# Four groups of hand-set places in a two-layer transformer kernel moved by up to one and a half steps

## The reference

```python
x = x + _L0_attn_ref(_layernorm(x), Mq, Mk, Mv)        # 8 heads, keys of 64, softmax over the queries
x = x + _L0_ffn_ref(_layernorm(x), w_gate, w_up, w_down)  # FP4 quantised inputs and weights, blocks of 16
x = x + _L1_attn_ref(_layernorm(x), w_qkv, ...)        # 16 heads of 16, norm of q and k per head
x = x + _L1_ffn_ref(_layernorm(x), W, b, R, A, B)      # top-2 routing over 8 low-rank experts
```

## Time and profile before

| | us |
|---|---|
| median of 3 runs | 2999.08 |
| lowest, highest | 2991.23, 2999.32 |
| the profiled execution | 2993.89 |
| its span, first to last instruction | 2992.1 |
| TensorE, VectorE, ScalarE, GpSimd busy | 2591.1, 2109.8, 1962.2, 1190.2 |
| HBM traffic over the span | 26 GB/s |
| mean granted TensorE clock | 0.967 of full speed |

### The profile page before, as it was taken

How to read it: one execution, slowest core, us unless ns; L and a number is a source line. 1 busy time by engine, 2 the same in 40 slices (tenths; PEclk the granted TensorE clock), 3 DMA queues, 4 the chain that set the end, 5 groups by cost and what they waited for, 6 DMA issues and landing times.

```text
span 2992.1 us, 115289 instructions
## 1 busy us (share of the span) xinstructions
PE 2591.1 (87%) x50174; PEld 1405.8 (47%) x50174; DVE 2109.8 (71%) x4321; ACT 1962.2 (66%) x3707; POOL 1190.2 (40%) x1677
## 2 busy tenths in 40 slices
PE   4766777999889988899889988899889988899697
PEld 3434554344644456444553456444553446444233
DVE  6778866766778478775778577785788667775433
ACT  2541355776668856787668766787668766687684
POOL 3653156224652166323652155421672246411210
PEclk9987999999999999999999999999999999999798
DMA  4212332324424252323423253152423243222310
GB/s 127 54 27 46 66 70 69 61 48 78 100 64 82 41 113 60 65 63 69 101 74 62 41 92 97 49 85 52 108 63 72 48 85 86 59 66 46 87 30 16
DMA packets 470171, 203.65 MB, mean 68 GB/s; under 512 B 283000, under 2 KB 459648, under 8 KB 469640
## 3 DMA queue, kind: packets, MB, share of 16 engines
q1 hardware_dynamic: 467960, 194.07, 31.3%
q10 hardware_dynamic: 1680, 1.85, 0.2%
HBM read 46.61 MB, written 32.51 MB: 26 GB/s over the span
## 4 chain that ended last, share of the span: by engine, by line
PE 43%; DVE 26%; issue 7%; ACT 7%; SPq 7%; DMA 6%; POOL 3%; DVEq 0%; POOLq 0%; ACTq 0%
PE pR L457 18%; PE pV L688 9%; DVE nmaxa L1215 7%; PE pS L457 6%; PE pS L648 5%; ACT ub L936 5%; PE pV L558 3%; PE pR L467 2%; SPq L1929 2%; SPq L2126 2%; DMA xT<-xhb 2%; SPq L2112 1%; DMA xT<-ua 1%; DVE ua L1118 1%; DMA ua<-ua 1%
## 5 line engine op out<-in xcount | busy, mean ns | idle before, releaser
L936 ACT ACTIVATE ub<-pS 128x512 f32<-128x512 f32 x2048 | 1048.0, 613 | 233.1 <-PE pS L648 232.4
L1215 DVE TENSOR_REDUCE nmaxa<-pS 128x1 f32<-128x1024 f32 x512 | 621.1, 1214 | 280.6 <-PE pS L457 279.2
L897 ACT ACTIVATE ua<-pS,nmaxa 128x1024 f32<-128x1024 f32 x384 | 427.7, 1114 | 457.0 <-DVE nmaxa L1215 454.5
L457 PE MATMUL pS<-ua 128*32 128x512 f16 x8192 | 546.6, 388 | 110.0 <-ACT ua L897 88.5
L688 PE MATMUL pV<-ub,vaug 128*17 128x512 f32 x4096 | 539.8, 600 | 13.4 <-DVE ub L1373 12.6
L1698 POOL TENSOR_TENSOR ua<-ua,rz 128x256 f32<-128x256 f32 x512 | 332.6, 651 | 485.8 <-DVE rz L1232 466.2
L648 PE MATMUL pS<-ub 50*128 50x512 f16 x1920 | 351.5, 385 | 26.6 <-DMA ub<-scr 11.5
L457 PEld LDWEIGHTS pS<-ua 128*32 128x32 f16 x8192 | 212.2, 98 | 280.2 <-ACT ua L897 123.7
L457 PE MATMUL pR<-wgu,xT 128*32 128x352 f16 x6144 | 282.7, 319 | 35.8 <-DMA xT<-ua 15.4
L648 PEld LDWEIGHTS pS<-ub 50*128 50x128 f16 x1920 | 95.8, 93 | 403.8 <-ACT ub L936 332.6
L558 PE MATMUL pV<-ua 128*32 128x128 f32 x6144 | 245.8, 280 | 36.9 <-DVE oTa L1226 22.9
(11 more groups left out here) (258 smaller groups left out, 4019.0 us busy)
## 6 DMA issues: line engine op xcount, KB each, us to landing
ua<-ua SPq DMA_DIRECT2D x384, 128.0 KB, 2.8
ub<-scr SPq DMA_DIRECT2D x264, 64.0 KB, 2.9
scr<-ub SPq DMA_DIRECT2D x30, 512.0 KB, 3.6
x<-in_L_attn_x SPq DMA_DIRECT2D x8, 1024.0 KB, 6.1
between<-x SPq DMA_DIRECT2D x7, 1024.0 KB, 5.9
ub<-between SPq DMA_DIRECT2D x7, 1024.0 KB, 6.1
out<-ub SPq DMA_DIRECT2D x7, 1024.0 KB, 5.5
ub<-scr SPq DMA_DIRECT2D x192, 32.0 KB, 1.9
```

Source lines behind the costliest of these rows:

```text
L457: i = e.matmul(dst[j:j + 32], w[:, j:j + 32], m, start=start, stop=stop)
L897: e.activation(EA[n % 4], pS[:, 1024 * (n % 2):1024 * (n % 2) + 1024], ACT.Exp, bias=nmaxa[:, n % 32:n % 32 + 1], accum_out=zz[:, n % 8:n ...
L936: e.activation(EB[(4 * n + hl) % 8], pS[:, 512 * hl:512 * hl + 512], ACT.Exp).then_inc(e1_in, 1)
L1215: e.tensor_reduce(nmaxa[:, n % 32:n % 32 + 1], pS[:, 1024 * (n % 2):1024 * (n % 2) + 1024], AXX, ALU.max, negate=True).then_inc(max0_in, 1)
```

## The change

Later projections of a pair stand 3.5 places apart instead of 3, the last of the four routing steps stands one place earlier, the first half of x's quantisation half a place earlier (the second half is left), and GpSimd's low halves 0.3 of a place later. No instruction is added or removed.

```diff
         P_AT = (2.1, 3.5, 6.5, 8.5)
-        R_AT = (19.0, 21.6, 25.2, 28.0)
+        R_AT = (19.0, 21.6, 25.2, 27.0)
 
         def project_at(pair, n):
-            return 16 * (pair - 1) + (0, 0, -1)[pair - 1] + 3 * n
+            return 16 * (pair - 1) + (0.0, 0, -1)[pair - 1] + 3.5 * n
...
         def fin_at(n):
-            return -21.5 + .85 * n if n < 20 else 3.3 + .8 * (n - 20)
+            return -22.0 + 0.85 * n if n < 20 else 3.3 + .8 * (n - 20)
...
             def moe_low(b, hf=None):
                 for tp in range(4) if b < NB - 2 else ():
-                    yield 14.4 + tp
+                    yield 14.7 + tp
                     lows("M", b, tp, xhm_[b])
```

## The result

| | before | after |
|---|---|---|
| median (lowest to highest), 8 executions each | 2994.68 (2991.13 to 2999.32) | 2975.91 (2973.26 to 2985.76) |
| the profiled execution, its span | 2993.89, 2992.1 | 2981.95, 2980.2 |
| mean granted TensorE clock | 0.967 | 0.966 |

The ratio of after to before is 0.9941 (95% interval 0.9926 to 0.9955): 0.6% faster, some 18 us, where the prediction had 3 us and a range from 2983 to 3009. A second set of 7 executions beside other runs of before gave 0.9934 (0.9911 to 0.9958). The profiled execution of after is 6 us slower than its median, so its trace shows 12 us of the gain.

What follows compares the result with a forecast made beforehand. TensorE, busy 87% of the span, was the engine whose idle time counted. -0.5 us a repeat times six gave -3 us, with 0 for batches 0 and 1: 2996 us as median from 2999.1, range 2983 to 3009.

Steps and rivals of the forecast that it cites:

- the one for batches 0 and 1: First two batches, beside weight preparation and a stretched grid: no change, with 1.5 us each way for each batch.
- low halves: GpSimd's low halves, place 14.4 to 14.7: no order changes in any batch, an empty edit at no cost.
- projections 2 and 3, to step 20: Pair 1's projections on TensorE: a 0.63 us bank wait loses its cause; estimate -0.15 us, bounds 0 and -0.63.
- steps 26 to 29, from step 20 to 36: Projection 7 and routing fill step 28's 1.27 us wait: -1.5 us, -1.3 with 0.2 lost before; bounds 0 and -1.9.
- base tile 0, to step 42: Projection 10 frees its bank late, delaying the base product by 0.9 us; with projection 11 behind the transposes, +0.85 us.
- crowd, to the sum of squares: VectorE from 1512.7 us: projection 11's low part and moved statistics raise the delay from +0.85 to +1.5 us.
- behind it, to the FFN's first matmul: x's block maximum moves ahead of step 49's maximum, where VectorE waits 0.87 us for scores: -0.5 us.
- the gain at steps 26 to 29 lives on: Rival: VectorE's stretch from 1512 absorbs the delays; -1.65 us a repeat, -10 for six, median about 2987.5; chance 0.30.
- The FFN's first matmul still waiting for the transpose by 2.5 us or more: Sign of being right: quantising sooner doesn't cut this 2.51 us wait, as SP's twenty query transfers stand in front.
- TensorE's waits for ScalarE in the stretch 1 to 2 us less: Sign of being right, in the attention 0 half: the wait of step 28's scores is gone.
- The slower rival: Projection 7 and routing meet banks not free, so the 1.27 us stay: +1.5 us a repeat, 3009; chance 0.22.
- The fills: SP: pair 2's k and pair 3's q fills fall behind key transfers, yet arrive before steps 32 and 48: cost 0.

Runs made afterwards that it cites:

- e13: New projection spacing (3.5) and sooner quantisation for batches 0 and 1 alone, against the kernel before; ratio 0.9971 (0.996 to 0.9982).
- e12: The kernel before with batch 1's fill of pair 2's k put behind the heads' input transpose, on SP's queue alone; ratio 1.0009 (0.9998 to 1.002).
- e4: Only GpSimd's low halves moved from 14.4 to 14.7, against the kernel before; ratio 0.9997 (0.9983 to 1.0011).
- e14: New spacing and sooner quantisation for batches 2 to 7 alone, plus the new last routing step, against the kernel before; ratio 0.9982 (0.9968 to 0.9996).
- e9: The changed kernel run once more, unaltered, against the kernel before; 2976.41 us, ratio 0.9934 (0.9911 to 0.9958).
- e11: The kernel before with the second ten query transfers behind the FFN input's transpose on SP's queue; ratio 0.9947 (0.9933 to 0.9962) of before.
- e7: The changed kernel with batch 1's projections back at a spacing of 3; ratio 0.9971 (0.9954 to 0.9989) of before.
- e5: Only routing's last step at 27 instead of 28, against the kernel before; ratio 0.9995 (0.9984 to 1.0006).
- e10: The changed kernel with the second ten query transfers behind the FFN input's transpose on SP's queue; 2964.25 us, ratio 0.9897 (0.9873 to 0.9922) of before.

## Why the prediction was wrong

**The step that failed** is the one for batches 0 and 1: "where weight preparation and a stretched grid stand beside, I take 0 with 1.5 us each way from the same terms". They gave -4 and -7 us (e13: 0.29%). The terms of a middle repeat don't hold there, because places stand in other orders: batch 1's attention 0 is stretched by 94/64, so the 1.5 places of projection 7 become 2.2 and take the fill past a transpose that it doesn't pass in batches 2 to 7. For batch 0 the runs show the size and not the mechanism. The prediction sorted SP's places and costed only a fill that comes late, for the scores behind it. It never asked what comes sooner once the fill is out of the way. Its sentence on the Trainium skill, "DMA: Bandwidth & Descriptors", anatomy of one DMA, had the mechanism: a wait on a semaphore happens on the issuing sequencer. The traces agree, the other way round from how it was used: the fill that waited for its low half until 410.0 us held back the transpose of another lane until 412.67. (The hold that the prediction saw in front of the FFN's transpose, by the same rule, was time of issuing.) From batch 1's start (320.5 us in before, 318.8 in after) the transpose is issued at 92.1 us behind the fill and 90.3 ahead of it, and the matmul that needs it starts at 97.7 and 95.1. The working had the stretched grid in view and gave it a round number; a look at batch 1's longest wait, 5.30 us, would have led to it. This order is one part of the -7 us: by itself it has some 2 us in e12's profile and nothing in e12's total. The others are the order at steps 36 to 44, some 1.9 us, and the clock.

**The middle repeats**, by the steps of the sum. Each measured number is how far the distance from the start of attention 0 moved over that piece, once in batch 4 of after against before, and once as the difference of means over batches 2 to 7 in the profiles of the table above (six old, five new):

| step | predicted, us | batch 4 | means |
|---|---|---|---|
| low halves | 0, empty | same order | e4 0.9997 |
| projections 2 and 3, to step 20 | -0.15 | -0.5 | -0.1 |
| steps 26 to 29, from step 20 to 36 | -1.3 | -1.8 | -1.5 |
| base tile 0, to step 42 | +0.85, wait of 0.9 | +1.0, wait of 0.63 | +1.0 |
| crowd, to the sum of squares | +0.65 | 0 | 0 |
| behind it, to the FFN's first matmul | -0.5 | -1.4 | -0.3 |
| a repeat | -0.5 | -4.2 | -0.9 |
| six repeats | -3 | | -5.4 (e14: 0.18%) |

In the means all but one were right in place and nearly in size; the one mis-sized term is the 0.65. Without it the prediction's own sum is -1.1. Nearly all of the -0.9 stands by the FFN's first matmul, so it doesn't come from the second half. The 0.65 us were counted item by item onto VectorE. Its timeline in after has a wait of 2.46 us ahead of step 42's maximum, and the moved statistics and projection 11's low half between that one and the next:

```profile
1500.62 1.23 DVE L1215 TENSOR_REDUCE nmaxa<-pS 128x1 f32<-128x1024 f32 x1 [2.46 <-PE pS L457]
...
1502.57 0.69 DVE L1095 SCALAR_TENSOR_TENSOR ua<-pR,ua 128x512 f16<-128x512 f32 x1
...
1503.87 1.23 DVE L1215 TENSOR_REDUCE nmaxa<-pS 128x1 f32<-128x1024 f32 x1
```

Step 43's scores come 1.25 us sooner than in before, like step 42's: the items fill the gap of 1.42 us and push nothing. That is the prediction's first rival, "the gain at steps 26 to 29 lives on", at half of its 1.65 us. "The FFN's first matmul still waiting for the transpose by 2.5 us or more" was wrong as a number: this wait was 0, 1.17, 0, 2.15 and 0.34 us in batches 3 to 7 of after, 0.45 to 4.43 in e9's, 2.17, 2.51, 1.47, 2.50 and 1.47 in before's. The prediction had named a shorter wait as a sign of being wrong, and it came. This wait is what is left over between two chains and changes from one execution to the next. That SP's twenty issues stand in front was right, and e11 shows that they are the bound: with ten of them moved the same kernel is 0.5% faster.

"TensorE's waits for ScalarE in the stretch 1 to 2 us less" was wrong too: 9.5 us in 11 pieces, before 8.4 in 12. The one wait went, and others grew.

**The slower rival**, by banks, didn't happen: step 28's scores came 0.4 us sooner relative to step 24's, in batch 4 and in the means, and the repeats are shorter in the mean. **The fills** cost nothing, as predicted: after has no wait of steps 16, 32 or 48 for a transfer in batch 4.

**The base.** Of the 20 us between forecast and result some 4 are before itself: the sum stood on three executions with a median of 2999.08, and eight of them have 2994.68.

## What to carry to other kernels

Where an order is set by places and the warm-up stages have a grid of their own, sort them separately: here the few repeats that differ from the steady state had the longest waits (5.30 us, against 2.5 in the steady ones), and an edit made for the others won more there. For a queue that issues transfers, ask of each moved item both what now waits behind it and what no longer does; in batch 1 one waiting group of four held the transpose behind it. And when a wait's cause is a queue, move the queue's order itself: the split of the queries, one more place in a list, gave nearly as much as all four edits.

## What the hardware showed

A long wait was paid twice here: with its own length, and with slower matmuls behind it. In before the 5.30 us at 418.26 lie in a stretch with a granted clock of 0.72 (stretches view, columns as above), and the 2.75 us for GpSimd at 462 us in one of 0.91; with shorter waits in after the first is 0.83 and the second 1.00.

```profile
412.00:424.00 12.00, 6.39 (x106) 3.44 (x110) 3.57 (x8) 3.39 (x6) 4.34 (x7) 0.72 0.54 79
452.00:470.00 18.00, 14.51 (x298) 9.57 (x298) 10.95 (x20) 10.81 (x18) 11.88 (x24) 0.91 0.47 126
```

```profile
410.00:420.00 10.00, 7.17 (x134) 3.86 (x130) 5.59 (x11) 3.42 (x6) 5.99 (x9) 0.83 0.54 108
447.00:462.00 15.00, 13.14 (x314) 9.18 (x306) 10.36 (x18) 10.24 (x17) 11.56 (x24) 1.00 0.51 136
```

In batch 1's whole repeat TensorE is busy for 327.25 us in before (PEclk 0.94) and for 323.85 in after (0.96), with the same instructions. So 3.4 of the 7.1 us between this pair are matmuls that ran faster, and 3.7 are shorter idle time. e7, with before's order in batch 1, has 327.66 us, and e9, the change again, 323.74. But e5, with before's order, has 324.58 at 0.95, so the clock doesn't follow from the order alone.

The pieces right behind the 2.75 us show the price. The scores took 1.79 us in before and 1.05 in after, the eight transposes 1.57 and 1.09:

```profile
462.40 1.57 PE L467 MATMUL pR<-ident,ub 128*128 128x128 f32 x8 [2.75 <-POOL ub L1820]
463.90 1.08 PE L558 MATMUL pV<-EA,ua 128*32 128x128 f32 x16
464.76 1.79 PE L457 MATMUL pS<-ua 128*32 128x512 f16 x16
```

```profile
455.72 1.09 PE L467 MATMUL pR<-ident,ub 128*128 128x128 f32 x8 [1.86 <-POOL ub L1820]
456.74 0.64 PE L558 MATMUL pV<-EA,ua 128*32 128x128 f32 x16
457.20 1.05 PE L457 MATMUL pS<-ua 128*32 128x512 f16 x16
```

The spread between executions of one kernel goes with the clock too. Of the 24 executions of before that stood beside e7 to e10, the three fastest (2980.64 to 2988.94 us) had a mean granted clock of 0.969 to 0.970 and the three slowest (3002.74 to 3008.81 us) 0.962 to 0.963. In the profiled execution of after, which is 6 us above its median, TensorE waits 2.00 us for a transpose at 1067.89 us, in batch 3's attention 0, and in the three stretches of 8 us from 1062 us on the granted clock is 0.91, 0.87 and 0.79. Which wait brings a fall of the clock, and which doesn't, is not shown.
